# An adaLN transformer block on one core: another beginning, two-input Vector operations, and the last batch's post work tile by tile

## The reference

```python
mod = (_silu(L0_c) @ L0_wmod).reshape(L0_c.shape[0], 6, 1, -1)
sa, ca, ga, sb, cb, gb = (mod[:, 0], mod[:, 1], mod[:, 2], mod[:, 3], mod[:, 4], mod[:, 5])
ga = (2 * (ga >= 0) - 1) * jnp.maximum(jnp.abs(ga), 0.25)
gb = (2 * (gb >= 0) - 1) * jnp.maximum(jnp.abs(gb), 0.25)
h = _layernorm(x, axis=-1) * (1 + ca) + sa
x = x + ga * attention(h)      # qkv = h @ W_qkv + b_qkv; softmax(q k) / sqrt(E) @ v; @ W_out + b_out
h = _layernorm(x, axis=-1) * (1 + cb) + sb
x = x + gb * ffn(h)            # quantise h and the weight, scales per 32; xd @ wd.T + bias
```

## Time and profile before

| | us |
|---|---|
| median of three runs | 292.14 (290.65 to 293.30) |
| the profiled execution's own time | 293.37 |
| its span in the trace | 291.6 |
| PE / DVE / ACT / POOL busy in the span | 259.6 / 235.6 / 218.1 / 191.6 |

### The profile page before, as it was taken

One profiled execution on the slowest core, in us unless ns is written; L12 is line 12 of the kernel. 1 busy time (PEld: TensorE's weight loads), 2 busy tenths in 40 slices (PEclk: granted clock), 3 DMA queues, 4 the chain that ended last, 5 costly groups with the idle time before them and its releaser, 6 DMA issues.

```text
span 291.6 us, 7402 instructions
## 1 busy us (share of the span) xinstructions
PE 259.6 (89%) x2538; PEld 169.7 (58%) x2538; DVE 235.6 (81%) x564; ACT 218.1 (75%) x439; POOL 191.6 (66%) x348
## 2 busy tenths in 40 slices
PE   2747789999999999999999999999999989899852
PEld 1425465666666666665656666666666656576431
DVE  4656396779899999999999999999989898952353
ACT  7469226797879797979797979797979787778510
POOL 2232307056979797978787878787888583837741
PEclk9985555999999999999999999999999999999965
DMA  5476663445444534436353545363535251100001
GB/s 140 122 215 180 186 170 125 120 139 133 128 125 137 157 120 137 139 94 180 110 174 109 167 112 158 103 180 99 181 95 181 80 176 47 39 22 24 18 0 36
DMA packets 21044, 35.44 MB, mean 122 GB/s; under 512 B 3312, under 2 KB 16768, under 8 KB 18960
## 3 DMA queue, kind: packets, MB, share of 16 engines
q1 hardware_dynamic: 20528, 34.33, 39.7%
q10 hardware_dynamic: 480, 0.66, 0.8%
HBM read 23.93 MB, written 10.52 MB: 118 GB/s over the span
## 4 chain that ended last, share of the span: by engine, by line
PE 65%; issue 8%; ACT 8%; DVE 7%; DMA 6%; SPq 3%; POOL 2%; POOLq 0%; DVEq 0%; ACTq 0%
PE ps_p L819 21%; PE ps_o L849 21%; PE ps_p L834 4%; PE ps_pre L871 4%; DMA x_all<-in_L_attn_x_dram 3%; PE ps_post L902 3%; ACT probs L566 3%; PE ps_post L916 3%; ACT hT L533 2%; DMA q_dram<-qk_parts 2%; PE ps_pre L878 2%; PE ps_pre L865 2%; ACT qk_parts L547 2%; PE ps_post L910 2%; DVE neg_max L718 2%
## 5 line engine op out<-in xcount | busy, mean ns | idle before, releaser
L718 DVE TENSOR_REDUCE neg_max<-ps_p 128x2 f32<-128x512 f32 x256 | 164.0, 680 | 21.1 <-PE ps_p L819 19.8
L566 ACT ACTIVATE probs<-ps_p 128x512 f32<-128x512 f32 x256 | 138.9, 597 | 17.1 <-PE ps_p L834 13.1
L819 PE MATMUL ps_p<-k_rows,q_rows 62*128 62x256 f32 x512 | 104.7, 324 | 6.8 <-DMA k_rows<-k_dram 4.3
L834 PE MATMUL ps_p<-q_rows,k_rows 64*128 64x256 f32 x512 | 101.7, 316 | 0.0
L819 PEld LDWEIGHTS ps_p<-k_rows,q_rows 62*128 62x128 f32 x512 | 74.9, 199 | 37.1 <-issue 15.6
L834 PEld LDWEIGHTS ps_p<-q_rows,k_rows 64*128 64x128 f32 x512 | 71.9, 189 | 3.5 <-ACT probs L566 2.4
L849 PE MATMUL ps_o<-probs,v_aug 128*32 128x256 f32 x1024 | 69.4, 389 | 0.3 <-ACT probs L566 0.3
L430 POOL CAST max_parts<-neg_max 128x16 fp32r<-128x16 f32 x32 | 6.3, 196 | 53.6 <-DVE neg_max L718 53.6
L849 PEld LDWEIGHTS ps_o<-probs,v_aug 128*32 128x32 f32 x1024 | 26.9, 110 | 20.3 <-issue 0.7
L871 PE MATMUL ps_pre<-hT,wqk_sb 128*128 128x256 f32 x56 | 20.1, 444 | 6.3 <-ACT qk_parts L547 4.3
L289 POOL TENSOR_SCALAR xh<-x,mv,rstd 128x128 f32<-128x128 f32 x30 | 23.6, 795 | 1.6
(11 more groups left out here) (98 smaller groups left out, 360.4 us busy)
## 6 DMA issues: line engine op xcount, KB each, us to landing
q_rows<-q_dram SPq DMA_DIRECT2D x32, 256.0 KB
k_rows<-k_dram SPq DMA_DIRECT2D x62, 128.0 KB
q_dram<-qk_parts SPq DMA_DIRECT2D x32, 128.0 KB, 2.3
modb<-mod_rows_dram SPq DMA_DIRECT2D x16, 256.0 KB, 3.4
k_dram<-qk_parts SPq DMA_DIRECT2D x30, 128.0 KB, 2.3
out_dram<-out_sb SPq DMA_DIRECT2D x16, 128.0 KB, 1.8
x_all<-in_L_attn_x_dram SPq DMA_DIRECT2D x1, 1536.0 KB, 9.9
q_rows<-maxT SPq DMA_DIRECT2D x64, 8.0 KB
```

The lines of the kernel that those rows point to most:

```text
L566: act.activation(probs[:, v % 2, u % 4, :], ps_p2[:, (16 * b + u) % P2_BANKS, :], ACT.Exp).then_inc(exp_done, 1)
L718: dve.tensor_reduce(neg_max[:, half, :, r, j], ps_p1[:, (16 * b + s) % P1_BANKS, :].rearrange("p (q k) -> p q k", q=QT), AX_X, ALU.max, ne ...
L819: ins = pe.matmul(ps_p1[:, (16 * b + s) % P1_BANKS, t * T:(t + 1) * T], q_rows[64 * r:64 * r + ROWS1, slot, i, t * P:(t + 1) * P], k_rows[ ...
L834: ins = pe.matmul(ps_p2[:, (16 * b + u) % P2_BANKS, t * T:(t + 1) * T], k_rows[64 * r:64 * r + ROWS2, slot, i, t * P:(t + 1) * P], q_rows[ ...
```

## The change

Three things. **The beginning**: ACT issues x of batch 0; `c_sb` is turned by TensorE before the exponential, so the silu is worked out on 128 partitions by 16; the modulation weight is loaded in two pieces and the qkv bias has a semaphore of its own; the high part of q and of k of batch 0 is stored without waiting for the low part; layouts go half by half, and the scores of heads 0 to 3 wait for half 0 alone (`laid_out[slot][half]`); the fills are spread over DVE (one), POOL (four) and ACT (three); x of batches 4 and 5 is a DMA of its own of 256 KB, and x of batches 6 to 15 (1,280 KB) is issued by SP at the end of step -1; `stats1` of batch 3 is taken at s = 13 of step -2, among the maxima. **Two-input operations**: `finish_stats` becomes two `tensor_tensor` (the mean times -1 into `nm`, the variance plus epsilon, both constants in SBUF), `block_scale` a `scalar_tensor_tensor` with a tile of floors, and the mean is added negated. **The last batch**: its post work goes tile by tile, each tile in PSUM banks of its own; `centre2` and `modulate2` become four `scalar_tensor_tensor`; batch 14's turning and linear layer move to `ps_p1`, between batch 15's norm and projection, and its result is added behind batch 15's statistics.

```diff
+        def ffn_psum(b):
+            return ps_p1[:, 0, 0:T] if b == LAST - 1 else ps_post
+        last_o = [ps_p2[:, t, 0:T] for t in range(QT)]
+        last_turned = [ps_p1[:, 1 + t, 0:P] for t in range(QT)]
+        last_y = [ps_pre[:, 0:P], ps_post[:, 0:P]]
+        last_f = [ps_p2[:, t, 0:P] for t in range(QT)]
...
+            sp.wait_ge(first_high, 1)
+            store_part(sp, 0, 0, (0,))
             sp.wait_ge(first_low, 1)
-            store_part(sp, 0, 0)
-            lay_out(sp, 0, 0)
+            store_part(sp, 0, 0, (1,))
+            lay_out(sp, 0, 0, (0,))
             lay_out(sp, 0, 1, (0,))
...
-            lay_out(sp, 1, 0)
-            lay_out(sp, 1, 1)
-            sp.dma_start(x_all[:, 4:NB, :, :], x_tok[:, 4:NB]).then_inc(x_in[3], 16)
+            for r in range(2):
+                lay_out(sp, 1, 0, (r,))
+                lay_out(sp, 1, 1, (r,))
+            sp.dma_start(x_all[:, 4:6, :, :], x_tok[:, 4:6]).then_inc(x_in[3], 16)
...
                 if has(b + 1):
                     place_max(b + 1, 1)
+                if b == -1:
+                    sp.dma_start(x_all[:, 6:NB, :, :], x_tok[:, 6:NB]).then_inc(x_in[4], 16)
...
-            def finish_stats(mv, ve, aggregated, value):
+            def finish_stats(mv, nm, ve, aggregated, value):
 
                 wait(dve, (aggregated, value))
-                return dve.tensor_scalar(ve[:, :], mv[:, :, 1], LN_EPS, None, ALU.add)
+                dve.tensor_tensor(nm[:, :], mv[:, :, 0], minus_one[:, :], ALU.mult)
+                return dve.tensor_tensor(ve[:, :], mv[:, :, 1], eps[:, :], ALU.add)
...
-                dve.tensor_scalar(sc64[:, :], amax[:, :], SUB / FP6_MAX, SUB * SCALE_FLOOR, ALU.mult, ALU.max
-                                  ).then_inc(sc_ready, 1)
+                dve.scalar_tensor_tensor(sc64[:, :], amax[:, :], SUB / FP6_MAX, floor64[:, :], ALU.mult, ALU.max
+                                         ).then_inc(sc_ready, 1)
...
+            def modulate_last():
+
+                wait(dve, (rstd2_ready, NB), modb_ready(LAST))
+                for n in range(QT):
+                    dve.scalar_tensor_tensor(xm2[:, n, :], x1[:, n, :], nm2[:, n:n + 1],
+                                             modb[:, LAST % MODB_RING, 2, :], ALU.add, ALU.mult
+                                             ).then_inc(last_scaled, 1)
+                for n in range(QT):
+                    wait(dve, (last_scaled, n + 1))
+                    dve.scalar_tensor_tensor(h2[:, n, :], xm2[:, n, :], rstd2[:, n:n + 1],
+                                             modb[:, LAST % MODB_RING, 1, :], ALU.mult, ALU.add
+                                             ).then_inc(last_h2_ready, 1)
...
-                    if s == 6 and in_steps(b + 5):
+                    if s == (13 if b == -2 else 6) and in_steps(b + 5):
                         stats1(b + 5)
...
-                if s == 0:
-                    wait(pe, (laid_out[b % RING], 96 * (b // RING + 1)))
+                if s == 0 or s == 4:
+                    wait(pe, (laid_out[b % RING][s // 4], 48 * (b // RING + 1)))
...
+                    if s == 4 and b - 1 == LAST:
+                        for t in range(QT):
+                            transpose_norm_last(t)
+                        transpose_hd(b - 2)
```

More of the change, by code:

```diff
@@ L58 @@
 FIRST = 2
+LAST = NB - 1
 HEAD = [8 * (u // 8) + 2 * (u % 4) + (u % 8) // 4 for u in range(16)]
@@ L484, in _ @@
             pool.memset(v_aug[:, :, :, 1, :], 0.0).then_inc(pads_ready, 1)
+            fill(k_rows, 1, 1.0)
+            fill(q_rows, 2, 0.0)
+            fill(k_rows, 2, 1.0)
             for b in STEPS:
@@ L566, in exponentials, with save_last @@
                 act.activation(probs[:, v % 2, u % 4, :], ps_p2[:, (16 * b + u) % P2_BANKS, :], ACT.Exp).then_inc(exp_done, 1)
+            def save_last(t, full, dst, src, saved, *before):
+                wait(act, (full, t + 1), *before)
+                act.activation(dst, src, ACT.Copy).then_inc(saved, 1)
             def save(b, full, reader, dst, src, saved, per=1):
@@ L603, in _ @@
                         save_v(b + 1)
-                    if s == 13 and has(b - 2):
+                    if s == 13 and b - 2 == LAST:
+                        for t in range(QT):
+                            save_last(t, last_hdT_full, hdT[:, t * P:(t + 1) * P], last_turned[t], last_hdT_saved,
+                                      (f_full, LAST))
+                    elif s == 13 and has(b - 2) and b - 2 != LAST - 1:
                         save(b - 2, hdT_full, f_full, hdT[:, :], ps_post[:, :], hdT_saved)
@@ L771, in _, with finish_last @@
+            def finish_last(t):
+                wait(dve, (last_f_full, t + 1), (x1b_ready, NB), (out_stored, 16 * LAST))
+                ins = dve.tensor_tensor(out_sb[:, t, :], last_f[t], x1b[:, t, :], ALU.add)
+                if t == QT - 1:
+                    ins.then_inc(out_ready, 1)
             for b in STEPS:
@@ L959, in _ @@
                         transpose_x(c, (maxT_saved, 2 * (b + 1)), (v_saved, 1))
-                    if s == 2 and has(b - 1):
+                    if s == 2 and b - 1 == LAST:
+                        for t in range(QT):
+                            transpose_o_last(t)
+                    elif s == 2 and has(b - 1):
                         transpose_o(b - 1)
@@ L965, in _ @@
                         project_qk(c, 1, k_full, ps_pre[:, :], (q_saved, 2 * (c - FIRST + 1)))
-                    if s == 4 and has(b - 1):
+                    if s == 4 and b - 1 == LAST:
+                        for t in range(QT):
+                            transpose_norm_last(t)
+                        transpose_hd(b - 2)
+                    elif s == 4 and has(b - 1):
                         transpose_norm(b - 1)
@@ L971, in _ @@
                         transpose_max(b + 1, 0, (k_saved, 2 * (c - FIRST + 1)) if pre else (maxT_saved, 2 * (b + 1)))
-                    if s == 8 and has(b - 1):
+                    if s == 8 and b - 1 == LAST:
+                        for t in range(QT):
+                            project_out_last(t)
+                        linear(b - 2)
+                    elif s == 8 and has(b - 1):
                         project_out(b - 1)
@@ L979, in _ @@
                         values(b, 2)
-                    if s == 12 and has(b - 2):
+                    if s == 12 and b - 2 == LAST:
+                        for t in range(QT):
+                            transpose_hd_last(t)
+                    elif s == 12 and has(b - 2) and b - 2 != LAST - 1:
                         transpose_hd(b - 2)
@@ L983, in _ @@
                         transpose_max(b + 1, 1, (v_saved, b + 2 if b >= 0 else 1), (maxT_saved, 2 * (b + 1) + 1))
-                    if s == 14 and has(b - 2):
+                    if s == 14 and b - 2 == LAST:
+                        for t in range(QT):
+                            linear_last(t)
+                    elif s == 14 and has(b - 2) and b - 2 != LAST - 1:
                         linear(b - 2)
```

253 lines of the change are left out of this document (181 added, 72 removed).

## The result

The changed kernel takes 284.35 us, the median of 4 runs (283.3 to 286.04), beside 292.72 us of the kernel before on the same chip: the ratio is 0.972, with a 95% interval of 0.967 to 0.977. The profiled execution took 283.3 us itself, with a span of 281.3 us; the one before took 293.37 and 291.6.

A forecast was written before the change was run, and what follows sets the result against it. TensorE and DVE bound the steps, waits the beginning, serial instructions the end. 3.0 + 2.03 + 2.33 - 0.8 + 0 + 2.25 = 8.8 us off 293.37 gives 284.6, as a median 283.3; range 280.5 to 287.0.

The forecast's parts named there:

- the first rival: Steps: two-input operations escape POOL, DVE 0.5 us a step shorter, TensorE's 0.18 us goes; 281.3 us, chance 0.16.
- the beginning's better bound: Up to the first scores: upper end of the expected gain, 4.9 us, where 3.0 was taken.
- First scores at 18.2: Beginning: layouts start near 12.4, scores of heads 0 to 3 need one half; 18.2 for 21.18, 3.0 us gained.
- The two stalls, 2.03 and 2.33 us: First scores to step 0: TensorE's waits for `hT` (2.03) and for a maximum behind x of batch 4 (2.33) go.
- the moved statistics: Before step 0: `stats1` of batch 3 moves between the maxima; 0.49 plus about 0.3, 0.8 us lost.
- The 1,280 KB hidden, with 1 us or more to spare: Steps 0 and 1: load through at 48, step 1's placing lands near 48.5, step 1 starts at 49.6 or later.
- Two-input operations worth 0: Every step: `ve` and `nm` still wait for POOL, first about 0.65 us, second 0.07 to 0.17; gain taken as 0.
- the third rival: Steps: second small operation falls behind POOL's second product, TensorE loses 0.4 to 0.65 us a step; 288.5 to 291.8, chance 0.06.
- TensorE's waits at late maxima, 0.18 us a step: Steps: all TensorE loses to late maxima; a full escape from POOL would give 11 times 0.18, 2.0 us.
- The end, 2.25 us: Last batch, `oT` to last sum: power earlier 1.0, four `scalar_tensor_tensor` 0.1, block scales 0.55, work by tiles 0.6.
- some 0.13 each time: End: cost of POOL's three batch 15 products beside the four `scalar_tensor_tensor`, leaving 0.1 us gained there.
- The clock: Up to step 0: TensorE's clock at 1.2 GHz; an earlier rise would gain more, left out of the sum.

The follow-up runs named there:

- e9: Changed kernel, but a batch's first scores wait for both halves of its layout again; 286.5 us, ratio 0.979 to the kernel before.
- e10: Changed kernel with ACT filling ring slots 1 to 3 in the old place, POOL none of them; 288.73 us, ratio 0.986 to the kernel before.
- e11: Changed kernel with x of batches 4 to 15 loaded in one DMA behind batch 1's layouts; 289.27 us, ratio 0.989 to the kernel before.
- e4: Changed kernel with the load of x 6 to 15 split, 8 to 15 loaded at step 1's end; 284.15 us, ratio 0.970 to the kernel before.
- e12: Changed kernel with first statistics' small operations in a quiet place, POOL's last-batch work moved, `wf_sc` with two inputs; 281.9 us, ratio 0.965 to the kernel before.
- e3: Changed kernel with the mean kept positive in `nm` and subtracted by POOL and DVE, not added negated; 292.63 us, ratio 1.000 to the kernel before.
- e5: Changed kernel without `nm`, the mean's own column subtracted by POOL and DVE; 285.03 us, ratio 0.973 to the kernel before.
- e6: Changed kernel with the first statistics' aggregation and small operations moved behind the second statistics' ones; 283.3 us, ratio 0.968 to the kernel before.
- e2: Changed kernel with `nm`, `ve` and `sc` computed by one-input operations with immediate constants; 285.14 us, ratio 0.974 to the kernel before.

## Why the prediction was right, point by point

The forecast was 283.3 us in a range of 280.5 to 287.0; the median is 284.35. It was 8.8 us of gain, and 8.37 lie between the medians. The beginning and the end came as argued; the steps came right by luck. (The lower end of the range does not follow from its own working: the first rival's 281.3 with the beginning's better bound, 4.9 in place of 3.0, is 279.4. Nothing hangs on it.) Of its steps:

- **First scores at 18.2.** They start at 18.20 in this profile, at 18.4 to 18.7 in the others with the same beginning. The layouts began at 12.19 us (12.4 expected), 1.24 before their old time, for which 1.0 was reckoned. Waiting for the whole costs 1.2 to 1.7 us (e9).
- **The two stalls, 2.03 and 2.33 us, less 0.8 for the moved statistics.** 3.56 in the sum, 3.76 measured. The sum is right, as both stalls went; no run measures the 0.8 by itself. But e10 and e11 show that they are not two terms: with either one back, 3.4 to 3.5 of the 3.76 us are gone. A stall's length before is its worth only beside everything else that moves. x of batches 4 and 5 lands at 29.06, not by 28, and DVE waits 0.20 us for it here and up to 0.7 in other runs: this was close.
- **The 1,280 KB hidden, with 1 us or more to spare.** Right for the total (e4), without the spare time. A sign that the prediction named as wrong, a wait for placed maxima at step 1, did appear, with 0.36 us and again in e12.
- **Two-input operations worth 0.** The number is right by luck: its reason was not. The step said that the first of the pair waits about 0.65 us and the second slips in for 0.07 to 0.17. With POOL as it was, both wait, 0.73 and 0.76 us, and the whole change is worth nothing (e3: 292.63 us). This is the third rival, to which the prediction gave 0.06 and 288.5 us or more. In the changed kernel they take 0.37 and 0.49 us, and not one of them 0.6 to 0.7 as the prediction's signs had it. What kept it away is an effect that stands nowhere in the prediction: POOL's normalising operation with add takes 448 ns in place of 796. Two of them stand ahead of the `qk_parts` pair, which now ends 0.35 us behind `nm`'s start, and `ve` meets a product of 0.46 us and not a subtraction of 0.7 us. The operand's sign was listed as an extra operation on DVE, and its effect on POOL's row was not asked for. The term is thus a sum of +0.75 us a step (e3 against e5) and -0.79 (the changed kernel against e3), and not one of small things.
- **TensorE's waits at late maxima, 0.18 us a step.** The quiet place gives 0.20 a step (e6), 2.0 us in ten steps, as named for a full escape; 1.05 of it is left between the medians.
- **The end, 2.25 us.** 1.90 in the two profiles. The power comes 1.07 us sooner behind `oT` (1.0 expected); from `h` to `sc`'s end 0.57 are gained (0.55; the 0.42 and 0.36 us that it is made of would be 0.78, but batch 14's sum began while `h` was still running), from there to the last sum 0.65 (0.6). The step that was mis-sized is "some 0.13 each time" for POOL's products beside the four `scalar_tensor_tensor`: from the power's end to `h`'s end are 2.09 us in place of 1.69, 0.4 lost and not 0.1 gained. The 0.13 came from one pair of rows in which the two met for part of an instruction; here three of DVE's four end 0.15 us behind the end of the POOL instruction that they meet, and take 0.53, 0.54 and 0.88 us in place of 0.34.
- **The clock.** Left out, rightly. From step 0's start to the first `oT` save are 15.62 us in the changed kernel's profile, 17.09 in e2 and 17.70 before, with the clock rising 3.7, 8.1 and 9.3 us into the step: the 2.08 us are the clock's, and most of them came from that one execution's early rise. 0.63 went again in the next two steps. e5 begins like the changed kernel and takes 17.70 us as before, so the removed stalls do not bring the rise forward by themselves; what does is open.

## What to carry to other kernels

Where two engines block each other's instructions, a small operation costs what it meets, not what it does. Changing the length of anything ahead of the meeting moved a step by 5% here, both ways, so look up in the timeline what stands beside it, and put it where the other engine waits. And when an edit alters the operands or the operation of an instruction, price the instruction itself again, also on the engine that seems to be hidden.
